# Experts' up-projection turned over: w1 stationary in plain fp32, a selected tile of it copied by ScalarE, w2 in memory of its own, VectorE unrolled

## The reference

```
h   = tokens(x)                                   # 5 representations, patches of 16x16, projected to 192
h   = h + attention(layernorm(h))                 # 12 heads of 64
xt  = layernorm(h)
idx = argmax(softmax(xt @ gate_w + gate_b))       # one of 8 experts for each token
for e in range(8):
    y   = gelu(xt @ w1[e] + b1[e]) @ w2[e] + b2[e]   # w1[e]: 192 x 768, w2[e]: 768 x 192
    out = where(idx == e, y, out)
return h + out
```

## Time and profile before

| | before |
|---|---|
| time, median of 3 runs (lowest to highest) | 322.96 us (322.77 to 323.25) |
| the profiled execution: its own time, its span | 322.51 us, 320.8 us |
| TensorE busy, matmuls | 275.4 us, 86% of the span, 3710 instructions |
| TensorE busy, weight loads | 248.8 us, 78% |
| VectorE busy | 172.6 us, 54% |
| ScalarE busy | 130.2 us, 41% |
| GpSimd busy | 64.2 us, 20% |
| granted TensorE clock, mean over the span | 0.899 of full speed |

### The profile page before, as it was taken

The page is one execution under the profiler, slowest core; times in us unless marked ns, Lnnn a source line. Parts: engine busy times, 40 slices in busy tenths (PEclk is TensorE's granted clock), DMA queues, the critical chain, the costliest instruction groups (busy, mean ns, idle before and its releaser), DMA issues.

```text
span 320.8 us, 9598 instructions
## 1 busy us (share of the span) xinstructions
PE 275.4 (86%) x3710; PEld 248.8 (78%) x3711; DVE 172.6 (54%) x491; ACT 130.2 (41%) x354; POOL 64.2 (20%) x102
## 2 busy tenths in 40 slices
PE   7939989999997999998999983657579999999981
PEld 7929969898796899787899772547458999988871
DVE  7974286644877345775445750136136665655540
ACT  3463544647554267445266431120024344244320
POOL 2540002130003220002220000010602344334221
PEclk9976999999998799996799967586769999999997
DMA  7987700302002101000000195291400221221100
GB/s 259 286 332 290 264 2 3 114 3 57 3 2 62 55 25 33 2 4 2 2 0 2 45 393 214 85 410 52 113 12 10 63 74 42 61 62 39 31 3 0
DMA packets 6033, 28.17 MB, mean 88 GB/s; under 512 B 1479, under 2 KB 2771, under 8 KB 4974
## 3 DMA queue, kind: packets, MB, share of 16 engines
q1 hardware_dynamic: 3902, 23.17, 20.0%
q0 software_dynamic: 1792, 4.04, 4.7%
q10 hardware_dynamic: 304, 0.44, 0.4%
HBM read 24.99 MB, written 3.34 MB: 88 GB/s over the span
## 4 chain that ended last, share of the span: by engine, by line
PE 67%; DVE 13%; DMA 6%; issue 6%; ACT 4%; POOL 2%; DVEq 1%; POOLq 0%; SPq 0%; ACTq 0%
PE psum L429 25%; PE psum L711 10%; PE psum L499 8%; DMA token_table<-rows 5%; PE psum L474 4%; PE psum L488 4%; PE psum L699 3%; PE psum L460 2%; PE psum L414 2%; PE psum L537 2%; DVE top L997 2%; PE psum L561 1%; DVE kT L998 1%; PE psum L422 1%; ACT w1B_part L783 1%
## 5 line engine op out<-in xcount | busy, mean ns | idle before, releaser
L1291 POOL TENSOR_SCALAR veps<-mv 96x1 f32<-96x1 f32 x24 | 8.2, 342 | 170.7 <-DVE mv L951 170.3
L429 PE MATMUL psum<-xn_hi,wq_parts 128*128 128x288 f32 x144 | 37.3, 328 | 4.0 <-DVE late_r L971 2.9
L711 PE MATMUL psum<-w2s,kT 128*128 x192 | 34.8, 331 | 2.4 <-DVE kT L1223 1.4
L711 PEld LDWEIGHTS psum<-w2s,kT 128*128 128x128 f32 x192 | 30.8, 190 | 4.7 <-issue 4.4
L499 PE MATMUL psum<-wo,oT 128*96 128x192 f32 x144 | 32.6, 390 | 0.7 <-ACT oT L819 0.7
L429 PEld LDWEIGHTS psum<-xn_hi,wq_parts 128*128 128x128 f32 x144 | 26.4, 203 | 5.0 <-issue 3.2
L499 PEld LDWEIGHTS psum<-wo,oT 128*96 128x96 f32 x144 | 27.8, 200 | 2.4 <-issue 0.8
L429 PE MATMUL psum<-late_r,wq_parts 128*128 128x288 f32 x96 | 29.1, 310 | 0.0
L429 PE MATMUL psum<-wq_parts,xn_hi 128*100 128x384 f32 x96 | 28.5, 350 | 0.0
L1342 POOL DMA_INDIRECT out<-oT,ids x16 | 16.1, 1007 | 54.9 <-DVE oT L1230 54.9
L911 ACT ACTIVATE qT<-qT 128x512 f32<-128x512 f32 (+1 forms) x32 | 15.1, 515 | 25.0 <-DVE qT L1216 24.9
(11 more groups left out here) (151 smaller groups left out, 586.4 us busy)
## 6 DMA issues: line engine op xcount, KB each, us to landing
w2s<-w SPq DMA_DIRECT2D x1, 4608.0 KB, 16.1
xb<-xT SPq DMA_DIRECT2D x4, 864.0 KB, 4.8
w1A_in<-w SPq DMA_DIRECT2D x3, 1024.0 KB, 7.4
w1B_in<-w SPq DMA_DIRECT2D x3, 1024.0 KB, 9.8
late<-b SPq DMA_DIRECT2D x1, 3072.0 KB, 11.8
token_table<-rows SPq DMA_DIRECT2D x3, 432.0 KB, 3.2
late<-w_proj SPq DMA_DIRECT2D x1, 960.0 KB, 4.9
kT<-b SPq DMA_DIRECT2D x1, 768.0 KB, 4.3
```

The lines of the kernel that those rows point to most:

```text
L429: mm = pe.matmul(dst, lhsT, rhs, start=(i == 0), stop=(i == len(parts) - 1))
L711: mm = pe.matmul(psum[:, 6, 0:D], hidT[i % 2][:, c * P:(c + 1) * P], w2s[:, bass.ds(e, 1), c, :], start=(c == 0), stop=(c == FCH - 1))
```

## The change

- **Experts' up.** w1[e] is stationary, in plain fp32, and the tokens are moving. For 6 pieces of 128 of the 768 hidden columns there is one product over the first 128 of the 192 inputs, and one over the other 64. The 64-row products go in pairs: one in the upper 64 rows of the array, one in the lower 64, into different banks. Each moves 128 columns. The result is already transposed (hidden x tokens), so turn_hidden, its copies and the addition of b1 by VectorE go; b1 is the bias of six gelu instructions of 128x128 on ScalarE, straight from PSUM into hidT.
- **w1's tile.** Before the products, ScalarE copies the expert's w1 and b1 (128 x 1158) from w1s to one of four w1_tile buffers, three tiles ahead. The addresses of `up` are then constants.
- **No rounding of w1:** round_w1 and split_w1 go, and so does the rounding of the tokens there; VectorE's take_x makes three plain copies.
- **DMAs.** w1 and b1 come in one load early on (4.6 MB), b2 after it; w2s has memory of its own and is loaded after block 0's rows are sent. b1's load of 3 MB with a copy for each partition goes.
- **VectorE's bodies** are written out four times (no loop). soften and normalise are reordered (soften_all), normalise(3) moves behind take_tokens(0) of the next body, and rank_tokens(b-1) moves behind take_xn_lo(1) of the next body (in body 3, to its beginning).
- **Body 3 on TensorE:** turn_rows(0) moves from before attend(3) to behind project_to(1), and a keep_clock(6) is added ahead of turn_rows(2). ScalarE's order there stays: take_rows(0), then take_attended(3).
- **Experts' order on TensorE:** up(i+1), turn_x(i+2), down(i); keep_clock(16) ahead of the first tile becomes keep_clock(30), and turn_x(1) comes before up(0).

The core of the diff:

```diff
@@ SP
-            load_w1(0)
...
             load_x(1)
-            sp.wait_ge(w1_here, 32)
-            load_w1(1)
-            sp.wait_ge(w1_here, 64)
-            sp.wait_ge(weff_ready[CHANNELS - 1], 1)
-            load_w1(2)
+            sp.dma_start(w1s[:, :, :], w1_b1).then_inc(w1_here, 16)
+            sp.dma_start(b2s[:, :, :], b2.partition_broadcast(P)).then_inc(b2_here, 16)
...
             for b in range(NB - 1):
                 if b + 2 < NB:
                     load_x(b + 2)
-                if b == NB - 2:
-                    complete(sp, product(VALUES[-1], b))
+                send_rows(b)
+                if b == 0:
+                    sp.wait_ge(weff_ready[CHANNELS - 1], 1)
                     sp.dma_start(w2s[:, :, :, :], w2).then_inc(w2_here, 16)
-                send_rows(b)
-
-            sp.wait_ge(av_full, NU * NB)
-            sp.dma_start(b2s, b2.partition_broadcast(P)).then_inc(b2_here, 16)
-            sp.dma_start(b1s, b1.partition_broadcast(P)).then_inc(b1_here, 16)
@@ TensorE, body 3
                     attend_next(2)
-                    turn_rows(0)
                     attend(3, b)
                     project_to(1)
+                    turn_rows(0)
                     project_to(2)
                     turn_rows(1)
                     gate(b, 0, 2)
+                    keep_clock(6, TR_BANK)
                     turn_rows(2)
@@ TensorE, experts
             def up(r, i):
-                pe.wait_ge(fx_ready, j + 1)
-                for lo, hi in ((0, 512), (512, FF)):
...
-                    split_product(psum[:, 2 * p2 + lo // 512, 0:hi - lo], [
-                        (fxA_hi[p2], wA), (fxA_lo[p2], wA), (fxA_hi[p2], wA_lo),
-                        (fxB[p2], wB), (fxB_lo[p2], wB)]).then_inc(up_full, 1)
+                j, p2 = r * 4 + i, i % 2
+                wA, wB = w1_tile[i % 4][:, 0:FF], w1_tile[i % 4][:, FF:FF + FF // 2]
+                pe.wait_ge(w1_ready, j + 1)
+                pe.wait_ge(fx_ready, j + 2)
+                for c in range(0, FCH, 2):
+                    at = c // 2 * P
+                    for k in range(2):
+                        pe.matmul(psum[:, 2 * p2 + k, at:at + SLOT], wA[:, (c + k) * P:(c + k + 1) * P], fxA[p2],
+                                  start=True, stop=False)
+                    for k in range(2):
+                        rows_ = slice(DB * k, DB * (k + 1))
+                        mm = pe.matmul(psum[:, 2 * p2 + k, at:at + SLOT], wB[rows_, at:at + P], fxB[p2][rows_, :],
+                                       start=False, stop=True)
+                mm.then_inc(up_full, 1)
...
             def four_tiles(r, last):
                 for i in range(4):
-                    turn_hidden(r, i)
-                    if not last or i < 2:
-                        up(r, i + 2)
-                    if not last or i < 1:
-                        turn_x(r, i + 3)
+                    if not last or i < 3:
+                        up(r, i + 1)
+                    if not last or i < 2:
+                        turn_x(r, i + 2)
                     down(r, i)
@@ ScalarE, bodies 0 to 2 (round_w1(b, 0), (b, 1), (b, 2) removed) and experts
+            def take_w1(r, i):
+                e = act.value_load(tile_expert[0:1, bass.ds(r * 4 + i, 1)], min_val=0, max_val=EXPERTS - 1)
+                act.copy(w1_tile[i % 4], w1s[:, bass.ds(e, 1), :].rearrange("p o f -> p (o f)")).then_inc(w1_ready, 1)
+
             def gelu(r, i):
+                j, p2 = r * 4 + i, i % 2
+                act.wait_ge(up_full, j + 1)
+                for c in range(FCH):
+                    ge = act.activation(hidT[p2][:, c * P:(c + 1) * P],
+                                        psum[:, 2 * p2 + c % 2, c // 2 * P:(c // 2 + 1) * P], ACT.Gelu,
+                                        bias=w1_tile[i][:, UP - FCH + c:UP - FCH + c + 1])
...
             def four_tiles(r, last):
                 for i in range(4):
+                    gelu(r, i)
                     if not last or i < 1:
+                        act.wait_ge(hid_ready, FCH // 2 * (r * 4 + i) + 1)
+                        take_w1(r, i + 3)
@@ VectorE (split_w1 removed; bodies unrolled)
+            def soften_all(b):
+                soften(0, b)
+                normalise(0, b)
+                soften(1, b)
+                soften(2, b)
+                normalise(1, b)
+                normalise(2, b)
+                soften(3, b)
...
                 take_tokens(0, product(("tok", 0), b))
+                normalise(3, b)
                 take_tokens(1, product(("tok", 1), b))
...
                 take_xn_lo(1, product(("xt", 1), b), NT * b + NT + 1)
+                if b > 0:
+                    rank_tokens(b - 1)
                 take_xn_lo(2, product(("xt", 2), b), NT * b + NT + 2)
...
-                soften(3, b + 1)
-                normalise(3, b + 1)
-                rank_tokens()
+                soften_all(b + 1)
```

More of the change, by code:

```diff
@@ L237, in build @@
         oTf = oT[:, :, :].rearrange("p k n -> p (k n)")
-        hid = [qTf[:, 0:FF], qTf[:, FF:2 * FF]]
         hidT = [kTf[:, 0:FF], kTf[:, FF:2 * FF]]
-        b2s = kTf[:, 2 * FF:2 * FF + EXPERTS * D].rearrange("p (e d) -> p e d", e=EXPERTS)
+        w1_tile = [late[:, i * UP:(i + 1) * UP] for i in range(4)]
+        fxA, fxB = [[qTf[:, (2 * i + k) * SLOT:(2 * i + k + 1) * SLOT] for i in range(2)] for k in range(2)]
         res = [oTf[:, i * D:(i + 1) * D] for i in range(4)]
@@ L693, in turn_hidden @@
-            def turn_hidden(r, i):
-                j = r * 4 + i
-                pe.wait_ge(hid_ready, j + 1)
-                pe.wait_ge(hidt_ready, j + 1)
-                pe.wait_ge(hidt_rest_ready, j + 1)
-                for c in range(FCH):
-                    mm = pe.transpose(psum[:, 4 + c // 4, (c % 4) * P:(c % 4 + 1) * P],
-                                      hid[i % 2][:, c * P:(c + 1) * P], ident[:, :])
-                    if c in (3, FCH - 1):
-                        mm.then_inc(hidt_full, 1)
+                j, p2 = r * 4 + i, i % 2
@@ L862, in body @@
                     return
-                round_w1(b, 0)
                 for g in range(3):
@@ L871, in body @@
                 take_rows(0)
-                heads(*QK[2:4])
-                round_w1(b, 1)
-                heads(*QK[4:5])
+                heads(*QK[2:5])
                 take_rows(1)
@@ L1067, in _ @@
             own(dve.tensor_copy(left[:, :], left_i[:, :]))
-            for g in range(NU):
-                soften(g, 0)
-                normalise(g, 0)
-            before_blocks = steps[0]
+            def soften_all(b):
[6 more added lines that the diff above has]
+                soften(3, b)
+            soften_all(0)
             def body(b, last):
-                steps[0] = 0
-                steps[1] = before_blocks + b * OWN_PER_BLOCK
                 lns = NT + b * 2 * NT
@@ L1135, in body @@
                     choose_experts()
-                    rank_tokens()
+                    rank_tokens(b)
                     return
@@ L1147, in body @@
                 take_xn_lo(0, product(("xt", 0), b), NT * b + NT)
-                split_w1(b, 0)
                 take_xn_lo(1, product(("xt", 1), b), NT * b + NT + 1)
+                if b > 0:
+                    rank_tokens(b - 1)
                 take_xn_lo(2, product(("xt", 2), b), NT * b + NT + 2)
-                take_o(0)
-                split_w1(b, 1)
-                finish_row(0)
-                take_o(1)
-                finish_row(1)
-                take_o(2)
-                finish_row(2)
-                split_w1(b, 2)
-                choose_experts()
-                soften(0, b + 1)
-                split_w1(b, 3)
-                normalise(0, b + 1)
-                soften(1, b + 1)
-                normalise(1, b + 1)
-                soften(2, b + 1)
-                normalise(2, b + 1)
-                soften(3, b + 1)
-                normalise(3, b + 1)
-                rank_tokens()
-                assert steps[0] == OWN_PER_BLOCK, steps[0]
-            with dve.Fori(0, NB - 1) as b:
-                body(b, False)
-            body(NB - 1, True)
+                for t in range(NT):
+                    take_o(t)
+                    finish_row(t)
+                choose_experts()
+                soften_all(b + 1)
+            for b in range(NB):
+                body(b, b == NB - 1)
             own(dve.tensor_tensor(steps9[:, :, :], filled[:, :].unsqueeze(2).to_broadcast([TT, EXPERTS, FULL]),
```

173 lines of the change are left out of this document (47 added, 126 removed).

## The result

| | before | changed |
|---|---|---|
| time, median of 4 runs each (lowest to highest) | 322.87 us (321.94 to 323.25) | 297.12 us (297.07 to 300.87) |
| the profiled execution: its own time, its span | 322.51, 320.8 us | 297.17, 295.4 us |
| granted clock over the span | 0.899 | 0.961 |
| TensorE busy, matmuls | 275.4 us | 270.2 us |

The ratio is 0.9235, with a 95% interval of 0.9161 to 0.9309: faster. (A ratio here is taken over paired rounds, so it need not be the quotient of the medians.) The forecast was 295.7 us in a range of 285 to 308. The total is 1.4 us off; the three terms behind it are not all that good.

The account below looks back on a forecast made before the run. TensorE, busy for 86% of the span, was taken as the bound, with time in its idling, half clock and own work. Gains of 12.0 + 8.6 + 6.2 = 26.8 us off 322.5 gave 295.7 us, range 285 to 308.

Parts of the forecast that it names:

- the three terms behind it: Gains forecast by stage: bodies 0 to 2 12.0 us, body 3 8.6 us, experts 6.2 us.
- `up` = 2.45 us: Experts: the new up of a tile takes 2.45 us, bounds 1.98 and 3.12.
- Only the middle two of four overlap: 3 x 0.11 a pair: Experts' up: four 64-row instructions of a pair take 3 x 0.11 us, 0.99 for three pairs.
- I take 0.15: Experts' up: six changes between 128-row and 64-row products cost 0.15 us a tile, within 0 to 0.48.
- bound of 3.12: Experts' up, upper bound in us: no overlap and all changes, 24 x 0.11 + 0.48.
- issue gaps of 0.2 a tile: Experts: issue costs 0.2 us a tile, 3.2 us over 16 tiles.
- half clock at the start: Experts' start: half clock costs 1.5 us, between 0 and 5.
- `up` is no cheaper: Rival, experts: pairs do not overlap and each mode change costs, 10.7 us more, 306.4 us; chance 0.17.
- pairs overlap fully: Rival, experts' up: 64-row pairs overlap fully, 7.5 us less, 288.2 us; chance 0.12.
- the forecast's 10.05 us for bodies 1 and 2: Bodies 1 and 2 get body 0's course and clock, saving 4.5 + 5.55 us.
- The chain worked out from the earlier trace: Body 3: attend(2) ends at 195.36, project(2) begins at 200.05 after a new ScalarE wait of about 1.1 us.
- the clock comes back with the wait gone: Bodies 1 and 2 and body 3: full clock once waits go; rival, clock stays low, 5 to 8 us more, chance 0.10.

Follow-up runs that it names:

- old_experts: Kernel before with everything of the change except the experts; rounding of w1, old up and b1's load stay: 309.48 us, ratio 0.9747.
- old_order: Changed kernel with VectorE's whole old order (soften and normalise in turn, normalise(3) and rank_tokens at the body's end), still without loop or rounding: 307.52 us.

## Why the prediction was right, step by step

**The total was right by 1.4 us with one term wrong by 6.6 and two by 2.7 and 1.6 the other way.** It is inside the range and on the right side, but the agreement of the sum is partly luck: 295.7 + 6.6 - 2.7 - 1.6 and 1.0 less for the opening and the tail is 297.0.

**Experts: the step that failed is "`up` = 2.45 us".** Measured 3.09. The working had three parts. 12 x 0.11 for the 128-row instructions was right (0.1115). "Only the middle two of four overlap: 3 x 0.11 a pair" was too cautious: both pairs overlap fully, 4 x 0.056 = 0.22 instead of 0.33, 0.3 us less a tile. "I take 0.15" for six changes is the term that was mis-sized: 3.09 - 12 x 0.1115 - 12 x 0.056 leaves 1.08 us for the changes in `up`, 0.93 more than forecast; the end of the sixth falls into turn_x (0.27 instead of 0.22). The scores' entry in the earlier trace rows shows only the first part of a change, about 0.09 us, so 0.08 a change was less than half of the 0.2. The Trainium skill, TensorEngine Tiling (Array Packing), Key Properties, says that a change of tiling mode drains TensorE; the trace agrees that a change costs time, about 0.2 us either way, and the 0.48 that I gave as its full price was nearer than my 0.15, though still less than half. That the bound of 3.12 held was luck: it had 2.64 for instructions that take 2.01 and 0.48 for changes that take 1.08. In all 16 x (0.64 + 0.05) = 11.0 us dearer than forecast. What came back: issue gaps of 0.2 a tile, taken as 3.2, measured as none, and half clock at the start, taken as 1.5, measured as none: keep_clock(30) holds it. That is 6.3 of the 6.6; the rest is in the two ends. The rival "`up` is no cheaper" had the total price right (10.7 us) and half of the mechanism: each change costs, but the pairs do overlap, as the rival "pairs overlap fully" had it. Its 306.4 did not come, because these two allowances (4.7 us) and the terms ahead of the experts (5.3) were too cautious.

**The scores were the right row for the overlap and the wrong one for the price of a change.** Their 48 quarter instructions overlap, and the halves do too. But 48 instructions share one entry and one exit, where four halves share as many. Counted with its two changes, an instruction costs 0.072 us in a group of twelve, 0.080 in eight and 0.107 in four. Four halves save 4 x 0.056 = 0.22 us by overlapping and pay 0.4 for the two changes.

**Bodies 0 to 2: direction and clock right, size small.** Forecast 41.35 in body 0, measured 41.07; I gave bodies 1 and 2 the course of body 0, and they are 40.2. Most of the difference is the rounding of w1, priced at 0.7 to 0.8 us a body and worth 2.0 at equal clock (old_experts against changed), 0.7 of it as a wait for the rows. The reason for that wait was half right: moving rank_tokens alone is worth nothing in body 2; VectorE's old order, with normalise(3) and rank_tokens at the end, is 0.7 to 0.8 of the 1.6 us, and the rounding by itself brings 0.7. rank_tokens fits under the projections in its new place, as said. That the forecast's 10.05 us for bodies 1 and 2 came is partly luck. With the sends swapped, body 2 has the code and the wait of before and took 43.08 us at clock 1.00, where it took 47.60 at 0.89 before: 4.5 us of clock came back with nothing changed in the body's work. Against that run, body 2 of the changed kernel gained 2.9 us. The prediction's "0.2% (0.6 us) is about what can be told" was far too narrow for the same reason.

**Body 3: 10.2 for 8.6.** The wait of 8.03 us went and the wait of 0.96 before project(2) came (forecast about 1.1). The chain worked out from the earlier trace rows has project(2) beginning 4.7 us after attend(2)'s end; measured 179.03 (179.77 less its wait of 0.74) to 183.93, 4.9. The end chain was 2.87 instead of 3.23. The rest, 1.4 us, lies ahead of it, where the same work ran less long at half clock (project(0) 3.53 us against 4.12, turn_probs behind it 0.99 against 1.40) than in the course of before that I carried over.

**Left open.** What brings half clock in body 3. It goes with w2's load in two kernels (0.65, 0.63), but project(1) took 2.19 us in the changed kernel and 3.87 in the one with ScalarE's order moved, with the same work before it, and project(0) took 3.53 and 2.16 in two kernels whose code up to there is the same. Nor does a wait decide it alone: with the sends swapped, waits of 1.7 and 1.6 us for the rows stood in bodies 1 and 2, and the clocks were 0.93 and 1.00. Waits of 0.7 and 0.8 us stood in body 2 of old_experts and of old_order at clock 1.00. So "the clock comes back with the wait gone" fits the sums and is not shown as a cause. VectorE's old order and the rounding bring 0.7 to 0.8 us of the wait each; whether they add up to the 1.6, and what the loop's turn-round adds, wasn't tried.

## What to carry to other kernels

Price a change of height by itself, and count the changes: a long row of small products shows the overlap and hides what it costs to enter and leave. Here a pair of 64-row products saved 0.11 us for every two instructions, and two changes cost about 0.4, so groups of four lost about 0.15 us each (a tile 0.46 us above full height) and a group of twelve won. Read the starts inside a group before saying that nothing overlaps in it; a sum over the group can't tell a missing overlap from a fixed cost. Where half-height products must stand between full-height ones, zeros in the idle half and no change of height were cheaper (2.68 against 3.09 us a tile), and one stationary block that serves both was no worse. And a term by term account is worth more than a total that fits: here the part that gave the change its name was a little dearer in its own stage, and the removed rounding that it made possible, two sends in the right order and a few transposes ahead of the experts gave the gain, beside a clock that scatters from run to run.

## What the runs showed that I had not expected

- A change between 128-row and 64-row products costs about 0.2 us in either direction, 0.1 in the group ahead of it and 0.1 in the group behind it.
- 64-row fp32 instructions of 128 columns on the two halves of the array start in pairs, 7 ns apart, and a pair takes 0.112 us, as long as one 128-row instruction. With the two changes counted in, four take 0.42 us, eight 0.64 and twelve 0.87.
- Thirty transposes whose result nobody reads, ahead of two waits for gathers (0.5 and 0.8 us), kept the clock of the next 8 us at 1.00; after sixteen (waits of 2.0 and 0.8 us) it was 0.51 for 13 us in which TensorE hardly paused, 5.2 us more.
